# A selection moved from VectorE to ScalarE and GpSimd, and the inner dimension of an expansion turned round, in a four-layer attention kernel

## Chip, cores and metric

The kernel runs on one core of a Trainium2 chip. The metric is the device time of one execution in microseconds (us), the median of some runs. Engines: PE is TensorE, DVE VectorE, ACT ScalarE, POOL GpSimd, SP SyncE.

## What is computed

For each of 32 batches of 128 x 1024 numbers there are four layers. The first and third are chunked self-attention layers over the context (8 heads, chunks of 64) with a residual and a layer normalisation. The second is a cross attention with LoRA weights (32 heads, width 1024). The fourth builds on geometry: for each of 1024 points of the context (first three channels of 128-channel rows, used as coordinates) it finds the 30 nearest of 1024, turns their relative coordinates into spherical ones, passes them through a three-layer perceptron with batch normalisation over everything, takes a softmax over the 30, and adds the weighted sum of the neighbours' features.

```python
idx = _knn(x_loc, k)
rel = pts[bidx, idx] - pts[:, :, None, :]
...
att = jax.nn.softmax(h[..., 0], axis=-1)
xk = x.transpose(0, 2, 1)[bidx, idx]
agg = jnp.einsum('bnkc,bnk->bnc', xk, att)
return x + agg.transpose(0, 2, 1)
```

## The kernel before

The program is written per engine, each with its own queue in hand-written order; engines meet at semaphores only. It has three stages.

**Main loop, 32 batches.** Each batch runs the first three layers. Their heads are worked in three blocks of four groups, n = 0 to 11. In a group PE computes scores, DVE takes a row maximum (`front`), ACT the exponentials, PE transposes the probabilities, ACT copies them out (`ET`), PE multiplies with the values, DVE normalises (`normalise`), PE transposes again (`outputs`), ACT copies that out (`output`, line 1008). After each block PE projects (line 758 in blocks 0 and 2, line 814 in block 1) and DVE adds the residual (lines 1369, 1405).

Between these steps DVE searches the 30 nearest neighbours of the batch (`search_round`, 32 of them, three operations of 1.2 us each on 1024 distances). The coordinates of the neighbours of the batch before are fetched in the same groups: an index is split into a low part (0 to 127) and a high part (0 to 7). A DMA spreads the low parts over all partitions, DVE compares them with the partition's number (`onehot`, line 1274), and PE multiplies the one-hot matrix with a table of coordinates (`fill`, line 636, 60 matmuls). That gives for each pair 3 coordinates x 8 possible high parts in the PSUM bank `MISC`. `consume` on DVE selects: it multiplies by the mask `hm` of the high part (line 1284) and sums over the 8 (line 1289) into `crd`. DVE does `consume` of group n-1 in group n, the last one behind the last group; PE's next `fill` waits for its `nb_used`.

POOL works in its own order: `tangents`, `norm_parts` (for the next batch's distances), `turn`, the split of the new indices, the coordinate table `ptab`, `relative`, `hm`, `sides`. Apart from `norm_parts` these are steps of the spherical coordinates.

**Perceptron.** Some 430 us, not touched.

**Aggregation, 32 batches.** The weighted sum over neighbours is computed by matmuls with one-hot matrices: an index is split into h (64 values) and l (16 values). For each half batch DVE forms weighted one-hots of l in `BA` (`weights`, line 1560, 16 operations). ACT expands them into block form `BD` (`blocks`, line 1220, four operations with a scale per partition, before each pair of chunks). DVE forms one-hots of h in `A1` (`onehots`, line 1569). PE multiplies both (`chunk`, line 918, eight chunks a batch, alternating over the banks SCA and SCB). ACT evacuates each chunk into `WT` (`columns`, line 1228), and PE forms the result from `WT` and the features, once for each half (`final`, line 931), behind chunks 1 (for the batch before) and 5. DVE adds the residual (`finish`). ACT's order is: expansion of the next pair, then the evacuations of this pair's two chunks. A chunk waits for its one-hots, its expansion, and the evacuation of the chunk two before.

```python
src = BA[half].rearrange("r l (h p) -> r h p l", h=2)[:, :, 32 * w:32 * w + 32, :]
for j in range(4):
    last = A(BD[v % 2][:, :, :, :, j], src, ACT.Copy, scale=blockmask[0:GROWS, j:j + 1])
```

## Time and profile before

| | us |
|---|---|
| median of 3 runs (8473.54 to 8476.95) | 8475.44 |
| the profiled execution | 8474.7 |
| its span, first to last instruction | 8472.9 |
| PE busy | 6946.1 |
| DVE busy | 6525.4 |
| ACT busy | 4626.7 |
| POOL busy | 1642.5 |
| mean granted clock of TensorE | 0.858 of 2.4 GHz |

Busy time is a sum over stages with different limits. The main loop takes the first four fifths of the span, the aggregation the last sixth; what a change is worth must be read in the stage where it lies. Matmuls are pipelined, so a busy PE isn't one at its peak.

### The profile page before, as it was taken

Reading aid. Unit: us, or ns where it says so; the run is one execution under the profiler, and the core shown is the slowest. Engines: PE = TensorE matmul, PEld = TensorE weight load, DVE = VectorE, ACT = ScalarE, POOL = GpSimd, SP = SyncE. Lnnn points to the kernel's source line nnn. Section 1 sums busy time; section 2 is a strip of 40 time slices with the busy share of each in tenths; the row PEclk is TensorE's granted clock in tenths of the full one; section 3 lists DMA queues with packets and bytes.
Section 4 is the critical chain, followed back from the end, with each engine's and each line's share of the span. In section 5 each row is a group of like instructions: output and inputs, shape, how many; then the busy total and the mean of one; then the engine's idle time right before and its main releaser. Section 6 shows DMA issues by size and latency. Waiting matters only on the chain.

```text
span 8472.9 us, 200463 instructions
## 1 busy us (share of the span) xinstructions
PE 6946.1 (82%) x79422; PEld 4984.0 (59%) x79422; DVE 6525.4 (77%) x9276; ACT 4626.7 (55%) x9523; POOL 1642.5 (19%) x1863
## 2 busy tenths in 40 slices
PE   8888888888888888888888888888888585888888
PEld 5555555555555555555555555555555332777777
DVE  5888888888888888888888888888888557666665
ACT  2444454554444444454444444444444225999999
POOL 1222222222222222222222222222222300010010
PEclk9888888888888888888888888888888797899999
DMA  2111111111111111111111111111111302222221
GB/s 97 57 54 54 54 54 54 58 56 54 54 54 54 57 58 59 64 54 57 57 57 57 54 54 54 54 54 57 57 57 55 101 16 54 55 55 55 65 55 49
DMA packets 295401, 481.05 MB, mean 57 GB/s; under 512 B 103250, under 2 KB 216034, under 8 KB 293698
## 3 DMA queue, kind: packets, MB, share of 16 engines
q1 hardware_dynamic: 240205, 372.00, 14.7%
q10 hardware_dynamic: 54133, 94.55, 3.5%
q8 instruction: 706, 11.57, 0.6%
q14 instruction: 357, 2.92, 0.1%
HBM read 393.25 MB, written 73.25 MB: 55 GB/s over the span
## 4 chain that ended last, share of the span: by engine, by line
PE 29%; DVE 27%; ACT 22%; issue 19%; DMA 1%; ACTq 1%; DVEq 1%; POOL 0%; SPq 0%; POOLq 0%
ACT arena L1220 8%; DVE m L1318 8%; DVE pd L1324 7%; PE SCA L814 5%; ACT S L1013 4%; ACT kexp L1055 3%; PE MISC L636 3%; DVE gat L1274 2%; DVE prod L1284 2%; DVE mx L1330 1%; PE TP L716 1%; PE TP L806 1%; PE SCB L654 1%; ACT reg L1065 1%; ACT reg L1228 1%
## 5 line engine op out<-in xcount | busy, mean ns | idle before, releaser
L1318 DVE MAX8 m<-pd 128x8 f32<-128x1024 f32 x1024 | 1249.1, 1220 | 207.2 <-ACT pd L988 94.2
L1322 DVE FIND_INDEX8 idx<-m,pd 128x8 uint32<-128x1024 f32 x1024 | 1248.3, 1219 | 0.0
L1324 DVE MATCH_REPLACE8 pd<-m,pd 128x1024 f32<-128x1024 f32 x768 | 928.5, 1209 | 0.0
L1569 DVE TENSOR_TENSOR gat<-maskT,con 120x2048 f32<-120x2048 f32 x256 | 580.9, 2301 | 295.6 <-PE SCA L918 281.0
L611 PE MATMUL PD<-arena 128*128 128x512 f32 x1028 | 695.8, 766 | 133.0 <-ACT pd L988 110.7
L636 PEld LDWEIGHTS MISC<-ptab,gat 128*128 128x128 bf16 x23400 | 667.7, 99 | 81.2 <-issue 44.4
L1013 ACT ACTIVATE S<-SCA,mx 128x64 f32<-128x64 f32 (+1 forms) x2560 | 571.4, 365 | 242.7 <-DVE mx L1330 242.7
L636 PE MATMUL MISC<-ptab,gat 128*128 128x24 bf16 x23400 | 664.7, 176 | 33.1 <-DVE gat L1274 23.1
L402 POOL CAST mb<-arena 96x1024 bf16<-96x1024 f32 x33 | 34.1, 1034 | 3078.8 <-ACT arena L978 3078.8
L1013 ACT ACTIVATE S<-SCB,mx 128x64 f32<-128x64 f32 (+1 forms) x2560 | 575.4, 399 | 0.0
L1330 DVE TENSOR_REDUCE mx<-SCA 128x16 f32<-128x1024 f32 (+1 forms) x192 | 235.1, 1225 | 429.1 <-PE SCA L739 420.6
L1220 ACT ACTIVATE arena<-S,con 120x1024 f32<-120x1024 f32 x256 | 542.6, 2375 | 17.4 <-DVE S L1560 17.4
L1220 ACT ACTIVATE arena<-pd,con 120x1024 f32<-120x1024 f32 x256 | 545.4, 2396 | 0.0
L988 ACT ACTIVATE pd<-PD,xxcol 128x512 f32<-128x512 f32 x514 | 355.4, 691 | 310.9 <-PE PD L612 305.1
L918 PE MATMUL SCA<-arena,gat 120*64 120x64 f32 x8192 | 325.6, 249 | 239.3 <-ACT reg L1228 130.2
L1008 ACT ACTIVATE OT<-TP 128x256 f32<-128x256 f32 x384 | 151.6, 395 | 657.8 <-PE TP L681 657.8
L783 PE MATMUL SCA<-reg,arena 128*128 128x128 f32 x4096 | 465.9, 276 | 35.6 <-ACT reg L1112 35.6
L783 PEld LDWEIGHTS SCA<-reg,arena 128*128 128x128 f32 x4096 | 459.8, 192 | 43.2 <-ACT reg L1112 43.2
L654 PE MATMUL SCA<-con,S 128*128 128x128 f32 x1536 | 234.4, 302 | 292.2 <-ACT S L1013 292.2
L750 PE MATMUL TP<-reg,ET 128*64 128x34 f32 x8192 | 389.7, 262 | 100.1 <-DVE on L1356 100.1
L750 PEld LDWEIGHTS TP<-reg,ET 128*64 128x64 f32 x8192 | 359.4, 180 | 179.2 <-issue 177.3
L918 PEld LDWEIGHTS SCA<-arena,gat 120*64 120x64 f32 x8192 | 307.0, 162 | 263.8 <-issue 263.8
(265 smaller groups left out, 15053.1 us busy)
## 6 DMA issues: line engine op xcount, KB each, us to landing
gat<-low_scratch SPq DMA_DIRECT2D x396, 640.0 KB, 4.3
arena<-in_ctx ACTq DMA_DIRECT2D x33, 512.0 KB, 4.0
maskT<-in_mask ACTq DMA_DIRECT2D x32, 512.0 KB
arena<-in_x ACTq DMA_DIRECT2D x32, 512.0 KB, 6.1
x_scratch<-arena ACTq DMA_DIRECT2D x32, 512.0 KB, 5.0
x3T_scratch<-arena ACTq DMA_DIRECT2D x32, 512.0 KB, 3.7
arena<-x3T_scratch SPq DMA_DIRECT2D x32, 512.0 KB, 7.1
arena<-x_scratch SPq DMA_DIRECT2D x32, 512.0 KB, 9.3
```

The lines of the kernel that those rows point to most:

```text
L611: mm(PD[:, :], ctx[:, t * P:(t + 1) * P], ctx[:, h * 512:(h + 1) * 512], start=True, stop=False)
L636: last = mm(place[:, o:o + 3 * NT], oh[n % NOH][:, kk * 256 + half * P:kk * 256 + (half + 1) * P], ptab[:, part, :, :].rearrange("p c t -> ...
L750: last = mm(TP[64 * half:64 * half + 64, (4 * b + pair) * 2 * VW:(4 * b + pair + 1) * 2 * VW], ET[:, o:o + 64], V2[:, (4 * g + 2 * b + hal ...
L783: last = mm(SC[0][:, c * P:(c + 1) * P], Wq[:, kc, c * P:(c + 1) * P], hT[:, kc, :], start=(kc == 0), stop=(kc == KC - 1))
L814: last = mm(SC[0][:, h * 512:(h + 1) * 512], OT[:, c * P:(c + 1) * P], Wo[:, c, h * 512:(h + 1) * 512], start=(c == 0), stop=(c == KC - 1))
L918: last = mm(SC[c % 2][64 * h:64 * h + 64, p * 64:(p + 1) * 64], A1[c % 2][:, h, p, :], BD[v % 2][:, h, c % 2 * 16 + p, :, :].rearrange("r ...
L1013: last = A(S[g % 2][:, r * keys:(r + 1) * keys], SC[g % 2][:, r * keys:(r + 1) * keys], ACT.Exp, bias=mx[g % 2][:, r:r + 1])
L1220: last = A(BD[v % 2][:, :, :, :, j], src, ACT.Copy, scale=blockmask[0:GROWS, j:j + 1])
L1318: step(V.max(m, buf[:, :]))
L1322: last = V.max_index(idx[:, t, 8 * r:8 * r + 8], m, buf[:, :])
L1324: step(V.match_replace(buf[:, :], m, buf[:, :], -3.0e38))
L1569: V.tensor_tensor(A1[c % 2], low[:, :, 16 * part:16 * part + 16].unsqueeze(3) .broadcast_to([GROWS, 2, 16, HV]), iota64[0:GROWS, :].unsque ...
```

## The change

It has two parts that don't depend on each other.

The first is in the aggregation. `BA` is stored with l innermost instead of outermost, and `BD` with (j, l) instead of (l, j). The expansion on ACT then reads and writes runs of 16 floats. The price of it moves: DVE's `weights` write with a step of 16 floats, the chunk's columns in PSUM come in another order, and ACT's evacuation reads PSUM with a step of 16 floats and writes runs of 64.

The second is in the main loop. `consume` leaves DVE. ACT copies group n's products from `MISC` into `prod` (`pick`, in group n, behind the exponentials of the next group), and POOL multiplies by `hm` and adds the 8 up in three steps, 4, 2 and 1 wide. POOL does groups 0 to 3 before `tangents`, 4 to 10 before `norm_parts`, and 11 behind it. `pick` waits until POOL has finished the group before. The layout of `prod` and `ptab` changes so that the 3 coordinates are innermost. In the tail behind the loop DVE still does the selection, in the new layout.

```diff
-        ptab = sb("ptab", [P, 3, 3, NT], bf16)
+        ptab = sb("ptab", [P, 3, NT, 3], bf16)
-        prod = sb("prod", [P, 2 * OHROWS, 3, NT])
+        prod = sb("prod", [P, 2 * OHROWS, NT, 3])
...
-        BD = [free[0:GROWS, n * UC * 64:(n + 1) * UC * 64].rearrange("r (h p l j) -> r h p l j", h=2, p=32, l=LV)
+        BD = [free[0:GROWS, n * UC * 64:(n + 1) * UC * 64].rearrange("r (h p j l) -> r h p j l", h=2, p=32, l=LV)
...
-        BA = [w[0:GROWS, :].rearrange("r (l c) -> r l c", l=LV) for w in (S01, pd01)]
+        BA = [w[0:GROWS, :].rearrange("r (c l) -> r c l", l=LV) for w in (S01, pd01)]
...
+            def consume(i, n):
+
+                if n == 0:
+                    pool.wait_ge(hm_ready, i + 1)
+                pool.wait_ge(nb_used, i * GROUPS + n + 2)
+                settle(pool)
+                count = [0]
+
+                def done(ins):
+                    count[0] += 1
+                    ins.then_inc(pick_step, 1)
+                    pool.wait_ge(pick_step, i * 3 * GROUPS + 3 * n + count[0])
+                    settle(pool)
+
+                pairs = slice(2 * n * OHROWS, 2 * (n + 1) * OHROWS)
+                done(G_.tensor_tensor(prod[:, :, :, :], prod[:, :, :, :], hm[:, pairs, :].unsqueeze(3)
+                                      .broadcast_to([P, 2 * OHROWS, NT, 3]), ALU.mult))
+                done(G_.tensor_tensor(prod[:, :, 0:4, :], prod[:, :, 0:4, :], prod[:, :, 4:8, :], ALU.add))
+                done(G_.tensor_tensor(prod[:, :, 0:2, :], prod[:, :, 0:2, :], prod[:, :, 2:4, :], ALU.add))
+                G_.tensor_tensor(crd[:, n * OHROWS:(n + 1) * OHROWS, :, :].rearrange("p k a c -> p (k a) c"),
+                                 prod[:, :, 0, :], prod[:, :, 1, :], ALU.add).then_inc(crd_done, 1)
...
                 pool.wait_ge(split_ready, i + 1)
+                for n in range(4):
+                    consume(i, n)
                 tangents(i)
+                for n in range(4, GROUPS - 1):
+                    consume(i, n)
                 norm_parts(i + 1)
+                consume(i, GROUPS - 1)
                 turn(i)
...
+                        def pick(n):
+                            act.wait_ge(nb_ready, i * GROUPS + n + NOH + 1)
+                            act.wait_ge(crd_done, i * GROUPS + n + 1)
+                            A(prod[:, :, :, :].rearrange("p k t c -> p (k t c)"), MISC[:, 0:6 * OHROWS * NT],
+                              ACT.Copy).then_inc(nb_used, 1)
...
                             if g < 3:
                                 exponentials(g + 1)
+                            pick(n)
                             if g == 0:
                                 expand(3)
                             if g:
                                 output(n - 1)
...
-                src = BA[half].rearrange("r l (h p) -> r h p l", h=2)[:, :, 32 * w:32 * w + 32, :]
+                src = BA[half].rearrange("r (h p) l -> r h p l", h=2)[:, :, 32 * w:32 * w + 32, :]
                 for j in range(4):
-                    last = A(BD[v % 2][:, :, :, :, j], src, ACT.Copy, scale=blockmask[0:GROWS, j:j + 1])
+                    last = A(BD[v % 2][:, :, :, j, :], src, ACT.Copy, scale=blockmask[0:GROWS, j:j + 1])
...
-                A(WT[half][:, :, c % 4 * 16:c % 4 * 16 + 16, :].rearrange("p l c j -> p c l j"),
-                  SC[c % 2][:, :].rearrange("p (c l j) -> p c l j", l=LV, j=4), ACT.Copy).then_inc(wt_done, 1)
+                A(WT[half][:, :, c % 4 * 16:c % 4 * 16 + 16, :].rearrange("p l c j -> p l (c j)"),
+                  SC[c % 2][:, :].rearrange("p (n l) -> p l n", l=LV), ACT.Copy).then_inc(wt_done, 1)
...
-                        if n:
-                            consume(i, n - 1, MISC)
...
-                    if l:
-                        consume(i, GROUPS - 1, MISC)
...
-                    last = V.scalar_tensor_tensor(BA[half][:, l, :], Lf[par][:, cols], float(l), attT[par][:, cols],
+                    last = V.scalar_tensor_tensor(BA[half][:, :, l], Lf[par][:, cols], float(l), attT[par][:, cols],
                                                   ALU.is_equal, ALU.mult)
```

## Rows read from the trace of the kernel before

**Rows 1.** The page's first line.

```profile
span 8472.9 us, 200463 instructions
```

**Rows 2.** One batch of the main loop, and most of the aggregation, by stretch: columns below.

```profile
core 0: us, PE busy (x) PEld busy (x) DVE busy (x) ACT busy (x) POOL busy (x), PEclk, DMA share, GB/s
...
3787.00:3992.00 205.00, 170.94 (x1793) 119.79 (x1792) 167.52 (x234) 99.86 (x268) 46.04 (x53) 0.85 0.17 56
...
7280.00:8440.00 1160.00, 956.26 (x18672) 880.95 (x18666) 756.96 (x1248) 1159.87 (x698) 103.84 (x140) 0.92 0.25 58
```

**Rows 3.** The chain that ended last, two batches: start, us, what.

```profile
3704.92 14.11 PE SCA L814 x32
3909.74 14.10 PE SCA L814 x32
```

**Rows 4.** Single lines: duration in ns, least, median, most; first and last start.

```profile
L1560 DVE SCALAR_TENSOR_TENSOR S<-maskT,TP x512: 272/279/289, 7174.4 to 8404.6; 120x128 f32<-120x128 f32 x171
...
L485 POOL TENSOR_TENSOR sph<-sph,arena x34: 1196/1199/1207, 288.2 to 6821.7; 128x480 f32<-128x480 f32 x34
...
L474 POOL TENSOR_TENSOR sph<-sph,arena x34: 1194/1712/1722, 165.0 to 6768.9; 128x480 f32<-128x480 f32 x34
...
L450 POOL TENSOR_TENSOR arena<-arena x34: 690/692/694, 107.5 to 6762.6; 128x240 f32<-128x240 f32 x34
```

**Rows 5.** The timeline of a quarter batch of the aggregation: start, us, engine, [idle before].

```profile
7803.00 1.14 ACT L1228 ACTIVATE arena<-SCA 128x1024 f32<-128x1024 f32 x1
7803.86 3.25 DVE L1560 SCALAR_TENSOR_TENSOR S<-maskT,TP 120x128 f32<-120x128 f32 x16
7804.29 3.16 PE L918 MATMUL SCA<-arena,gat 120*64 120x64 f32 x64 [3.13 <-ACT arena L1228]
7804.84 8.40 ACT L1220 ACTIVATE arena<-pd,con 120x1024 f32<-120x1024 f32 x4
...
7809.72 0.48 PE L931 MATMUL PD<-arena,kexp 64*128 64x256 f32 x1
...
7813.00 1.09 ACT L1228 ACTIVATE reg<-SCA 128x1024 f32<-128x1024 f32 x1
...
7816.82 2.08 PE L918 MATMUL SCA<-arena,gat 120*64 120x64 f32 x64
7818.74 2.04 PE L918 MATMUL SCB<-arena,gat 120*64 120x64 f32 x64
```

**Rows 6.** Groups of the main loop, ACT, from 96 to 6650 us.

```profile
L1055 ACT ACTIVATE kexp<-reg,con 128x256 f32<-128x256 f32 x1024 | 447.5, 581 | 0.0
...
L978 ACT ACTIVATE arena<-PD 96x512 f32<-96x512 f32 x64 | 37.7, 588 | 8.8 <-PE PD L597 8.8
```

**Rows 7.** Groups of the aggregation: busy us, mean ns, idle before.

```profile
L1569 DVE TENSOR_TENSOR gat<-maskT,con 120x2048 f32<-120x2048 f32 x242 | 548.7, 2300 | 272.4 <-PE SCA L918 258.6 <-PE SCB L918 13.4
```

**Rows 8.** The timeline of DVE and PE in group 6 of the main loop.

```profile
3889.41 0.65 DVE L1284 TENSOR_TENSOR prod<-MISC,hm 128x480 f32<-128x480 f32 x1
3890.09 0.65 DVE L1289 TENSOR_REDUCE crd<-prod 128x60 f32<-128x480 f32 x1
3890.66 1.22 DVE L1318 MAX8 m<-pd 128x8 f32<-128x1024 f32 x1
...
3895.36 2.38 PE L806 MATMUL TP<-reg,ET 128*128 128x33 f32 x16 [2.33 <-DVE on L1356]
```

**Rows 9.** The timeline of POOL, the last of the norm parts.

```profile
3761.11 1.03 POOL L406 CAST mb<-arena 32x1024 bf16<-32x1024 f32 x1 [0.17 <-POOL arena L405]
```

**Rows 10.** The timeline of ACT and PE in group 3.

```profile
3834.11 0.52 ACT L1008 ACTIVATE OT<-TP 128x256 f32<-128x256 f32 x1
...
3839.97 1.98 PE L758 MATMUL SCA<-OT,WL 128*128 128x512 f32 x4 [0.47 <-ACT OT L1008]
```

**Rows 11.** The timeline of ACT and PE in groups 9 to 11.

```profile
3744.52 1.29 ACT L1024 ACTIVATE arena<-arena 128x1024 f32<-128x1024 f32 x1
...
3756.70 1.92 PE L750 MATMUL TP<-reg,ET 128*64 128x34 f32 x32 [2.03 <-DVE on L1356]
...
3768.08 3.78 PE L758 MATMUL SCA<-OT,WL 128*128 128x512 f32 x4 [0.47 <-ACT OT L1008]
```

17 lines of the change are left out of this document (9 added, 8 removed).

## The prediction

> **What bounds the kernel now.** I read the page first: the execution spans 8472.9 us [rows 1], and its slices change their look once, late. The views by stretch split it into two stages that matter. In one batch of the main loop PE is busy 171 of 205 us, DVE 168, ACT 100, POOL 46. In the aggregation at the end ACT is busy 1159.9 of 1160 us and PE 956 [rows 2]. The chain of waits then gives the pace of the main loop: the 14 us projection of line 814 starts 204.82 us after that of the batch before [rows 3]. Its chain passes from DVE to PE to ACT and back several times in a batch, so a microsecond taken from one engine counts only where that engine is the late one. The aggregation (from 7174 us [rows 4] to the end, 1298 us) is simpler: the timeline of ACT repeats the same thing every 10.0 us, four expansions (line 1220) and two evacuations (line 1228), without a gap, while PE stands idle 3.1 us before each second pair of chunks, waiting for ACT [rows 5]. There ACT alone sets the time, 40.0 us for a batch.
>
> **Part 1, runs of 16 in the expansions.** Four expansions of 120x1024 take 8.16 us from their start to the evacuation behind them, 2.04 us each or 2.0 ns an element [rows 5]. What sets line 1220 apart is its pattern: it reads single floats 1 KB apart and writes them 16 bytes apart. The same operation with both sides contiguous (a copy from SBUF to SBUF with a scale per partition, line 1055) does 256 elements in 447.5/1024 = 0.437 us [rows 6], so four of them 1.75 us with the fixed part counted four times. The other ACT operation of 1024 elements in this stage, the evacuation, takes 0.92 us (1.84 for two [rows 5]). After the change both sides of the expansion are runs of 16 floats. I take 1.05 us, nearer to the row of the same size. Below 1.5 us nothing hangs on it, as the walk below shows. The bounds are 0.92 and 2.04 (the pattern wasn't the cause).
>
> The Trainium skill's page "SBUF — State Buffer", section Specifications (TRN2), says that a 16-byte line needs at least two accesses in a row for full bandwidth and that every step to a new line costs. The trace agrees: one access per line goes with 2.0 ns an element. By that rule the new expansions run at full rate, which gives the same sum.
>
> The evacuation now reads PSUM in single floats 64 bytes apart and writes runs of 64. No row shows such a read on ACT. Bounds: 0.92 as now, and twice that, 1.84, which is the penalty that line 1220 shows. ACT then needs 16 x 1.05 + 8 x 0.92 = 24.2 us a batch, or 31.5 with the upper one; with 1.5 us for an expansion it would be 31.4. The same page gives PSUM lines of only 8 bytes, which speaks against this edit; by it the evacuations would take the upper value, and the batch about 32.5 us in place of 31.6.
>
> The weights of DVE (line 1560) now write single floats 64 bytes apart. A group of 16 takes 3.25 us [rows 5]; if the write costs double, about 5.4 us.
>
> So what is late next? I walk one batch from the start of chunk 0, with PE at its higher clock. A chunk takes 1.92 us, the final products with the transposes 7.1 us [rows 5], a one-hot of DVE 2.27 us [rows 7], and up to 0.15 us for each handover (evacuation over at 7804.14, chunk at 7804.29 [rows 5]). A one-hot may start only when the chunk two before is done, and chunk c needs one-hot c. Chunk 1 starts at 2.25, final and transposes run 4.2 to 11.4, chunk 2 starts at 11.45, chunk 3 at 13.4. One-hot 4 runs 13.55 to 15.85, chunk 4 starts at 15.95, chunk 5 (one-hot 5 ends at 18.1) at 18.2, the other final runs 20.2 to 27.05, chunk 6 starts at 27.1, chunk 7 at 29.05; the next one-hot 0 runs 29.2 to 31.5, and the next chunk 0 starts at 31.6. PE is busy 8 x 1.92 + 2 x 7.1 = 29.6 of the 31.6 us, DVE 8 x 2.27 + 6.5 = 24.7 and some small ones, ACT 24.2. The weights fall into both finals (2.2 to 7.6, 18.1 to 23.5 even at the double cost), where DVE has over 3 us spare, so they cost nothing; without that cover they would cost 2 us each. The longest gap of PE is 0.6 us. Now it idles 3.1 us and the chunk behind takes 3.16 us instead of 2.08 [rows 5]; the granted clock of the stage is 0.92 [rows 2], so such chunks run in part at the lower of its two levels (1.2 in place of 2.4 GHz). This goes too, and my walk counts on it. Gain 40.0 - 31.6 = 8.4 us a batch, times 32: 269 us. Bounds: 31.0 us (all handovers free) and 34 us (clock still falls once a batch): 288 and 192 us.
>
> **Part 2, the selection.** Removed from DVE: 12 pairs of multiply and reduce in a batch, 0.65 us each, 1.25 us from the start of the first to the next operation [rows 8], 15 us a batch. Added on ACT: 12 copies of 480 floats out of PSUM. The nearest row is the 512 wide copy of line 978, 0.59 us [rows 6]; I take 0.55 us, 0.5 in a stream. Added on POOL: a multiply of 480, then adds of 240, 120 and 60, each waiting for the one before (0.17 us from one to the next [rows 9]). POOL multiplies 480 in 1.20 us and 240 in 0.69 [rows 4], so 2.1 ns an element beside 0.18 us: 1.2 + 0.69 + 0.44 + 0.31 and three handovers of 0.17, 3.2 us. Upper bound 4.2: the 480 multiply of line 474 takes 1.71, and the broadcasts could add as much again. That is 38 us a batch on a POOL that is busy 46 of 205: it fits.
>
> A new wait comes with it: ACT may fill prod for group n only when POOL is done with n-1. Behind that wait in ACT's queue stands the evacuation of the last head output, and behind it PE's output projection. The groups of the three attention blocks:
>
> Block 0 (groups 0 to 3). PE sets the pace; DVE gains little. The copy of group 2 can start at 3834.1, where line 1008 stands now [rows 10]; it and the handovers last to 3834.9, POOL's 3.2 us end at 3838.1, and the copy of group 3, whose matmuls are done by then, ends at 3838.9. Outputs 2 and 3 then follow one another on ACT and PE, and the projection of line 758, now at 3839.97 [rows 10], starts 0.3 us later. Bounds: 0.2 gained, 1.3 lost (4.2 us on POOL). I take 0.3 lost.
>
> Block 1 (groups 4 to 7). Here DVE is late: PE waits 2.33 us for its normalisation [rows 8]. Two selections lie on that path, 2.5 us. PE's own work behind (values, transposes, line 636) lets through about 2.3. A one-hot of DVE can meet POOL's multiply here. I take 2.0, bounds 1.0 and 2.5. What follows is PE's 14 us projection, so this carries on.
>
> Block 2 (groups 8 to 11). The copy of group 8 lies on ACT's path, in front of the expansion and the square of line 1024 [rows 11], and costs 0.5 us. PE waits 2.03 us for DVE at 3756.70; that wait shrinks by 1.25 - 0.5 = 0.75, and then PE's own chain up to the output projection limits, with about 0.3 more from the last normalisation. The selection in front of line 1369 goes as well, and the projection becomes the late one. I take 1.3. Bounds 0.5 and 3.5: the projection takes 3.78 us here and 1.98 in block 0 [rows 10, 11], after a wait of PE that the change shortens.
>
> POOL's moved steps: the norm parts (8 us, now over at 3762.1 [rows 9]) have to wait for selection 10, to about 3762. They are then done at 3770, and PE asks for them behind the projection of line 758, at 3771; selection 11 and the last turn end at 3776, and POOL is next needed by the last search at 3778. Cover of 1 to 2 us, so nothing; at 4.2 us a selection this cover is gone and it costs up to 0.5 us. The tangents wait for DVE's reciprocal between selections 3 and 4, 10 us before group 4 has data: nothing. The tables written in another order cost the same. The tail's 12 selections stay on DVE.
>
> Sum: 2.0 + 1.3 - 0.3 = 3.0 us a batch, 96 us over 32.
>
> **The total.** 8472.9 - 269 - 96 = 8107.9 us of span; the profiled execution had 1.8 us beside its span, 8109.7, and the median of the runs stands 0.7 above that execution: 8110 us.
>
> **The rivals.** (a) POOL and DVE get in each other's way. Line 474 on POOL takes 1.19 us at best and 1.71 usually [rows 4], so something holds it. With 38 us more of POOL's work among the groups, a one-hot of DVE in block 1 could start 1 us late and ACT's copies later: the lower bounds of the three blocks, 1.0 + 0.5 - 1.3 = 0.2 us a batch, 6 us in place of 96, 8200 us. Against it: only 2 or 3 of the 12 selections meet a one-hot where DVE is late. Chance 0.16. The Trainium skill, same page, section "SBUF: two separate sides", makes this an exclusive lock for the whole instruction, against DVE's operations with two SBUF inputs or in a fast mode; by it the time would go towards the 8200 of this rival.
> (b) The clock stays up in blocks 1 and 2, because PE's waits of 2 us shrink: the upper bounds, 2.5 + 3.5 + 0.2 = 6.2 us a batch, 8474.7 - 269 - 198 = 8008. Against: PE's other waits in the loop stay. Chance 0.12.
> (c) The aggregation takes 34 us a batch, by slower evacuations and a falling clock together: 8110 + 77 = 8187. Against: PE's longest gap in the walk is 0.6 us. Chance 0.10.
> (d) The expansions don't get faster, since something else holds them: 8474.7 - 96 = 8379. Against it stand the contiguous copies [rows 6]. Chance 0.04.
> (e) Slower than before: POOL's selection lasts so long that ACT waits for it in every block. Two copies follow one another by 3 us in block 0, and by my placing of them by about 6 in the others. To eat 269 + 96 us, 11.4 us a batch and 3.8 a block, a selection must last some 5 + 3.8 = 8.8 us against my 3.2; from there it decides. At 10 us the time would be 8474.7 + 3 x 1.2 x 32 = 8590. Chance 0.03.
> My forecast (8110, own range 8050 to 8170) has 0.55.
>
> **How the numbers follow.** The range 7990 to 8220 takes in the forecast, (a), (b) and (c), and leaves out (d) and (e). 0.2% is 17 us, about what a measurement of this kernel can tell. Only (e) is slower; faster 0.96, same 0.01, slower 0.03.
>
> **What the profile after would show.** Line 1220 near 1.0 us each and ACT with gaps in the aggregation; PE near 9 tenths there, granted clock near 1, batch 31.6 us. In the loop, the projection of line 814 every 201.8 us, copies of 0.55 us on ACT, four POOL operations summing to 3.2 us. I would be wrong if line 1220 stays near 2 us, if one-hots start behind POOL's operations, or if ACT's copies wait for POOL in block 1 or 2.

## The result, and the profile after

The changed kernel takes 8265.39 us (median of 4 runs, 8259.28 to 8271.05) beside 8476.19 for the one before: ratio 0.9751, interval 0.9734 to 0.9768, 211 us less. I had forecast 8110 with a range of 7990 to 8220, so the direction was right and the size was not: 155 us of the forecast gain are missing. The profiled execution took 8271.05 us.

First the page: the span, the busy times and the granted clock over 40 slices.

```profile
span 8269.3 us, 204463 instructions
...
PE 6884.4 (83%) x79422; PEld 4925.1 (60%) x79422; DVE 6179.9 (75%) x8508; ACT 4307.4 (52%) x9907; POOL 2685.8 (32%) x3399
...
PEclk9888888888888888888888888888888779899999
```

DVE lost 346 us of work and ACT 319, POOL took on 1043. Where the time stands is read from two rows: the weights of the aggregation (their first start divides the stages) and the projection of line 842 (814 before), each with durations in ns and its first and last start.

```profile
L1591 DVE SCALAR_TENSOR_TENSOR S<-maskT,TP x512: 359/388/416, 7113.1 to 8214.0; 120x128 f32<-120x128 f32 x171
...
L842 PE MATMUL SCA<-arena,OT x1024: 590/592/1061, 217.7 to 6529.7; 128*128 128x512 f32 x171
```

The aggregation begins at 7113.1 instead of 7174.4 [rows 4], so all that lies ahead of it gained 61 us, where 96 were forecast. From there to the end it takes 8269.3 - 7113.1 = 1156.2 instead of 1298.5, 142 us less, where 269 were forecast. So 127 us are missing in the aggregation and 35 in the main loop (together 162 of span against the forecast 8107.9; 155 by the medians).

The windows over most of the aggregation, which answer to [rows 2]:

```profile
core 0: us, PE busy (x) PEld busy (x) DVE busy (x) ACT busy (x) POOL busy (x), PEclk, DMA share, GB/s
7260.00:8200.00 940.00, 834.51 (x16712) 760.87 (x16710) 707.83 (x1120) 639.41 (x626) 144.04 (x130) 0.95 0.27 64
```

ACT fell from all of the stage to 68%, PE rose from 82% to 89%: as forecast, PE is the late engine now. The groups of ACT and DVE there (busy us, mean ns, idle before):

```profile
L1255 ACT ACTIVATE arena<-pd,con 120x1024 f32<-120x1024 f32 x210 | 223.8, 1139 | 0.0
...
L1263 ACT ACTIVATE arena<-SCB 128x1024 f32<-128x1024 f32 x52 | 53.1, 1021 | 45.0 <-PE SCB L946 45.0
...
L1600 DVE TENSOR_TENSOR gat<-maskT,con 120x2048 f32<-120x2048 f32 x210 | 486.1, 2353 | 146.7 <-PE SCA L946 138.2 <-PE SCB L946 8.6
L1591 DVE SCALAR_TENSOR_TENSOR S<-maskT,TP 120x128 f32<-120x128 f32 x416 | 97.0, 387 | 0.0
```

The time from one batch's transposes to the next alternates: 33.10 us, then 36.7 to 41.1 (from 7265.50 on: 40.79, 33.10, 39.11, 33.10, 38.63, and so on to the end), 35.9 in the mean. The walk gave 31.6 for all. The timeline of a quick batch shows the first part of the difference (start, us, engine, idle before):

```profile
7743.29 4.49 DVE L1600 TENSOR_TENSOR gat<-maskT,con 120x2048 f32<-120x2048 f32 x2 [0.97 <-PE SCA L946]
7743.78 1.21 PE L946 MATMUL SCB<-arena,gat 120*64 120x64 f32 x35
7745.92 2.08 PE L946 MATMUL SCA<-arena,gat 120*64 120x64 f32 x64 [0.92 <-DVE gat L1600]
...
7745.97 4.26 ACT L1255 ACTIVATE arena<-pd,con 120x1024 f32<-120x1024 f32 x4
7748.02 2.08 PE L946 MATMUL SCB<-arena,gat 120*64 120x64 f32 x64
```

Ahead of chunks 0 and 4, so once in four chunks, PE idles 0.92 us for a one-hot. The first of the two one-hots takes 2.29 us by itself and ends at 7745.58, and the chunk starts 0.34 us later, not 0.10 as in the walk. The same wait stood in the trace of the kernel before, at one chunk 4:

```profile
7722.22 2.29 DVE L1569 TENSOR_TENSOR gat<-maskT,con 120x2048 f32<-120x2048 f32 x1 [0.96 <-PE SCA L918]
...
7724.84 2.08 PE L918 MATMUL SCA<-arena,gat 120*64 120x64 f32 x64 [0.92 <-DVE gat L1569]
```

At chunk 1 of the quick batch PE waits once more, for another reason. One-hot 0 holds up an operation of POOL that took 0.74 us in the median before, and this one then holds up one-hot 1, which ends after 2.82 us instead of 2.29:

```profile
7759.40 5.03 DVE L1600 TENSOR_TENSOR gat<-maskT,con 120x2048 f32<-120x2048 f32 x2 [3.28 <-PE SCA L946]
7759.87 2.40 POOL L592 TENSOR_TENSOR maskT<-ctxT 120x256 f32<-120x256 f32 x1 [0.18 <-POOL ctxT L591]
...
7764.66 2.09 PE L946 MATMUL SCB<-arena,gat 120*64 120x64 f32 x64 [0.55 <-DVE gat L1600]
```

The start of a slow batch, 20 us before the first of these timelines, shows the second part:

```profile
7721.06 5.03 DVE L1600 TENSOR_TENSOR gat<-maskT,con 120x2048 f32<-120x2048 f32 x2 [3.51 <-PE SCA L946]
7721.22 2.71 POOL L592 TENSOR_TENSOR maskT<-ctxT 120x256 f32<-120x256 f32 x1 [0.18 <-POOL ctxT L591]
...
7726.17 2.19 PE L946 MATMUL SCA<-arena,gat 120*64 120x64 f32 x36 [3.41 <-DVE gat L1600]
7728.98 1.76 PE L946 MATMUL SCA<-arena,gat 120*64 120x64 f32 x28 [0.62 <-issue]
7730.52 3.12 PE L946 MATMUL SCB<-arena,gat 120*64 120x64 f32 x64
```

PE idles 3.41 us where it idled 0.92, breaks off in the middle of the chunk without a wait ("issue"), and the next chunk takes 3.12 us instead of 2.08, at the lower clock. The timeline names DVE's one-hot as what ended the 3.41 us, but that one-hot had ended at 7723.35, 2.8 us before the chunk starts. This is where TensorE's loop of two batches jumps back. All 14 jumps look like this: PE idles 3.2 to 4.8 us (3.9 in the mean), breaks off after 36 of 64 matmuls (0.8 in the mean), and these batches take 39.0 us in the mean.

In the main loop, the groups of POOL's selection (lines 509 to 513), ACT's copy and DVE's one-hots, over the stretch 2400 to 6500 us:

```profile
L509 POOL TENSOR_TENSOR prod<-prod,hm 128x480 f32<-128x480 f32 x242 | 256.1, 1058 | 1845.8 <-ACT prod L1041 1738.7 <-issue 107.2
L511 POOL TENSOR_TENSOR prod<-prod 128x240 f32<-128x240 f32 x242 | 182.4, 754 | 43.2 <-POOL prod L509 43.2
L512 POOL TENSOR_TENSOR prod<-prod 128x120 f32<-128x120 f32 x242 | 111.3, 460 | 43.2 <-POOL prod L511 43.2
L513 POOL TENSOR_TENSOR crd<-prod 128x60 f32<-128x60 f32 x242 | 87.5, 362 | 43.2 <-POOL prod L512 43.2
...
L1041 ACT ACTIVATE prod<-MISC 128x480 f32<-128x480 f32 x242 | 154.6, 639 | 60.5 <-POOL crd L513 32.4 <-PE MISC L664 28.0
...
L1309 DVE TENSOR_SCALAR gat<-gat,con 128x2560 bf16<-128x2560 bf16 x243 | 243.9, 1004 | 0.0
```

The selection on POOL takes 1.06 + 0.75 + 0.46 + 0.36 and three handovers of 0.18, 3.17 us: the forecast 3.2. The copy takes 0.64 us, not 0.55. But a one-hot takes 1004 ns in the mean, and ACT waits for POOL. The one-hots of the kernel before, same stretch:

```profile
L1274 DVE TENSOR_SCALAR gat<-gat,con 128x2560 bf16<-128x2560 bf16 x240 | 210.8, 878 | 0.0
```

Single one-hots show how. The timeline in block 2 (groups 8 to 11) of one batch:

```profile
2902.26 1.04 POOL L509 TENSOR_TENSOR prod<-prod,hm 128x480 f32<-128x480 f32 x1 [5.72 <-ACT prod L1041]
2902.28 1.70 DVE L1309 TENSOR_SCALAR gat<-gat,con 128x2560 bf16<-128x2560 bf16 x1
...
2903.48 1.06 POOL L511 TENSOR_TENSOR prod<-prod 128x240 f32<-128x240 f32 x1 [0.18 <-POOL prod L509]
2904.07 1.66 PE L664 MATMUL MISC<-ptab,gat 128*128 128x24 bf16 x60
```

POOL starts 0.02 us ahead, and DVE's 0.88 us one-hot takes 1.70; then POOL's add of 0.69 takes 1.06, since the one-hot is running. Over all 396 one-hots the median is 878 ns and the longest 1742, and the 174 that have no POOL operation beside them take at most 0.89 us; of the 12 in this batch ten took 0.88 and two 1.70 and 1.73, and PE stands behind them. The Trainium skill's page "SBUF — State Buffer", section "SBUF: two separate sides", calls the port pair of the two engines an exclusive lock, held for the whole instruction by whichever starts first; the trace agrees, with 0.88 against 1.70 us here.

The same happens at a place that the forecast didn't look at, the last step of the first layer norm. The changed kernel's timeline:

```profile
2994.58 1.83 DVE L1414 TENSOR_SCALAR X<-X,mv,rstd 128x1024 f32<-128x1024 f32 x1
...
2994.66 1.20 POOL L475 TENSOR_TENSOR sph<-sph,arena 128x480 f32<-128x480 f32 x1 [0.18 <-POOL arena L472]
```

and that of the kernel before:

```profile
2826.57 0.81 DVE L1383 TENSOR_SCALAR X<-X,mv,rstd 128x1024 f32<-128x1024 f32 x1
...
2826.74 1.72 POOL L474 TENSOR_TENSOR sph<-sph,arena 128x480 f32<-128x480 f32 x1 [0.18 <-POOL arena L471]
```

There POOL's product began 0.17 us behind DVE's step and waited (1.72); now it begins 0.08 us behind DVE's recorded start and DVE waits (1.83). It does so in every batch: 1826 to 1840 ns in all 32, against 811 to 814 before. This is the 1.71 against 1.19 us of line 474 in [rows 4], seen from the other side.

How a batch of the main loop divides, in means over 29 or 30 batches from the timelines of PE (a stretch in us, and the granted clock in it; of the last two columns more below):

| stretch | before | after | `ln_first` | `copy_only` |
|---|---|---|---|---|
| line 842 to block 2 | 32.3 | 32.6 | 32.7 | 33.4 |
| block 2, to its output projection | 31.1 (0.87) | 32.9 (0.73) | 32.3 (0.75) | 29.8 (0.76) |
| to block 0 | 41.2 | 41.0 | 41.0 | 40.9 |
| block 0, to its output projection | 30.7 (0.69) | 28.0 (0.82) | 28.7 (0.79) | 28.2 (0.78) |
| that projection and the first layer norm, to line 811 | 13.6 | 14.9 | 13.9 | 14.7 |
| line 811 to block 1 | 21.1 | 22.0 | 21.5 | 22.1 |
| block 1, to line 842 | 34.8 (0.76) | 31.6 (0.81) | 32.0 (0.80) | 29.3 (0.91) |
| sum | 204.8 | 203.0 | 202.1 | 198.4 |

Block 0 gained 2.7 us and block 1 gained 3.2, but block 2 lost 1.8 and the stretches around line 811 lost 2.2. In the kernel before, every step from the fourth on was 204.7 to 204.9 us; now they run from 197.6 to 207.7. The loop has also become uneven from one trace to the next. Seven kernels here (the changed one, `p2_only`, `agg_pe3`, `agg_dve3`, `agg_flat`, `onehot_12`, `three_buf`) have this same main loop, and their aggregations begin at 7096 to 7129 us. So a difference of less than some 30 us in the main loop can't be read from one trace, while a stretch of the table can: the projection with the layer norm has 14.9 to 15.0 us in all seven.

### The profile page after: what moved, and what is told of

It is laid out like the page before. It is cut to its first block, busy times and chain, and to the rows that moved or that the text cites. A ratio compares the mean times of both kernels' runs of the same rounds, so it can differ in the third digit from the quotient of the medians.

```text
span 8269.3 us, 204463 instructions
## 1 busy us (share of the span) xinstructions
PE 6884.4 (83%) x79422; PEld 4925.1 (60%) x79422; DVE 6179.9 (75%) x8508; ACT 4307.4 (52%) x9907; POOL 2685.8 (32%) x3399
## 4 chain that ended last, share of the span: by engine, by line
PE 54%; DVE 16%; ACT 15%; issue 10%; POOL 2%; DMA 1%; ACTq 1%; DVEq 0%; SPq 0%; POOLq 0%
ACT S L1047 6%; PE SCA L842 6%; PE PD L959 5%; PE SCA L811 4%; PE MISC L664 4%; PE SCA L946 3%; DVE m L1353 3%; ACT kexp L1090 3%; PE TP L834 3%; DVE pd L1359 3%; PE SCB L946 2%; PE PD L639 2%; PE SCA L682 2%; PE SCA L786 2%; PE TP L778 2%
## 5 line engine op out<-in xcount | busy, mean ns | idle before, releaser
L1353 DVE MAX8 m<-pd 128x8 f32<-128x1024 f32 x1024 | 1249.3, 1220 | 210.8 <-ACT pd L1016 99.0
L509 POOL TENSOR_TENSOR prod<-prod,hm 128x480 f32<-128x480 f32 x384 | 406.1, 1057 | 2928.8 <-ACT prod L1041 2762.2
L639 PE MATMUL PD<-arena 128*128 128x512 f32 x1028 | 660.8, 730 | 149.7 <-ACT pd L1016 127.5
L811 PE MATMUL SCA<-reg,arena 128*128 128x128 f32 x4096 | 500.7, 288 | 35.6 <-ACT reg L1147 35.6
L682 PE MATMUL SCA<-con,S 128*128 128x128 f32 x1536 | 276.4, 340 | 281.4 <-ACT S L1047 281.4
L842 PE MATMUL SCA<-arena,OT 128*128 128x512 f32 x1024 | 471.7, 621 | 0.0
L682 PEld LDWEIGHTS SCA<-con,S 128*128 128x128 f32 x1536 | 232.6, 177 | 372.7 <-ACT S L1047 341.7
L1365 DVE TENSOR_REDUCE mx<-SCB 128x16 f32<-128x1024 f32 (+1 forms) x192 | 234.6, 1222 | 286.5 <-PE SCB L767 252.4
L1090 ACT ACTIVATE kexp<-reg,con 128x256 f32<-128x256 f32 x1024 | 445.4, 572 | 0.0
L1309 DVE TENSOR_SCALAR gat<-gat,con 128x2560 bf16<-128x2560 bf16 x396 | 397.4, 1003 | 60.3 <-DMA gat<-low_scratch 60.3
L561 POOL TENSOR_SCALAR hm<-hif 128x240 bf16<-128x240 f32 x256 | 398.6, 1709 | 8.0
```

Of the source, the lines that this page charges most:

```text
L639: mm(PD[:, :], ctx[:, t * P:(t + 1) * P], ctx[:, h * 512:(h + 1) * 512], start=True, stop=False)
L682: last = nc.tensor.transpose(SC[g % 2][:, b * 512 + j * P:b * 512 + (j + 1) * P], S[g % 2][:, b * 512 + j * P:b * 512 + (j + 1) * P], ident)
L811: last = mm(SC[0][:, c * P:(c + 1) * P], Wq[:, kc, c * P:(c + 1) * P], hT[:, kc, :], start=(kc == 0), stop=(kc == KC - 1))
L842: last = mm(SC[0][:, h * 512:(h + 1) * 512], OT[:, c * P:(c + 1) * P], Wo[:, c, h * 512:(h + 1) * 512], start=(c == 0), stop=(c == KC - 1))
L1090: last = A(kexp[:, o:o + 256], kT[:, g * 256:(g + 1) * 256], ACT.Copy, scale=headmask[:, h:h + 1])
L1353: step(V.max(m, buf[:, :]))
```

## The experiments

The ratios stand against the kernel before. Medians are of 4 runs (5 for `ln_first`, 6 for `best_ln`).

**1. Each part alone.** `p1_only` is the kernel before with the layouts of `BA`, `BD` and the two ACT views; `p2_only` is the changed kernel with these undone.

> The kernel before with the expansion part alone. If the two parts simply add, the aggregation keeps its 142 us gain and the main loop its old pace of 204.8 us: 8476 - 142 = 8334 us. If the moved selection also disturbs the tail or the start of the aggregation, this kernel gains more than 142 us, towards 8320.

> The kernel before with the selection part alone. If the parts add: 8476 - 61 = 8415 us, the projection of line 842 every 203.1 us on the mean with unequal steps (197.7 to 207.7), and 40.0 us a batch in the aggregation. If the uneven steps came from the other part of the change, which has no work in the loop, they are gone here.

Measured: 8329.53 us (0.9826, 0.9810 to 0.9843) and 8421.05 (0.9937, 0.9920 to 0.9953). The parts are worth 147 and 55 us, and 147 + 55 = 202 of 211: they add, to within the spread of `p2_only` (8413 to 8439). The miss has a part in each stage, then.

**2. Whose jump makes the slow batch?** `agg_pe3` gives TensorE a loop over six batches in the aggregation, `agg_dve3` gives it to DVE.

```diff
-            with pe.Fori(0, NB // 2 - 1) as pair:
-                for odd in (1, 0):
-                    aggregate(pair * 2 + (2 - odd), odd, pair + (1 - odd))
+            with pe.Fori(0, (NB // 2 - 1) // 3) as three:
+                for m in range(3):
+                    for odd in (1, 0):
+                        aggregate(three * 6 + (2 * m + 2 - odd), odd, three * 3 + (m + 1 - odd))
```

> The changed kernel, with six batches instead of two in the body of PE's aggregation loop, so 5 jumps instead of 15, and DVE's loop as it was. Theory J (PE's own jump is what costs 3.4 us of gap, a break of 0.6 us and chunks at the lower clock, some 5.4 us each): 10 jumps less, 8265 - 54 = 8211 us, and the slow chunk 0 appears only once in six batches. Theory D (DVE's jump costs it: PE waits for one-hots that come late): 8265 us, no change. Theory C (the clock alone falls once a pair whatever the loop is): 8265 us.

> The same with DVE's loop unrolled threefold and PE's as it was. Theory J: 8265 us, no change. Theory D: 8211 us. Theory C: 8265 us.

Measured: 8271.62 (0.9761, 0.9740 to 0.9782) and 8270.96 (0.9767, 0.9739 to 0.9795). Neither gained. With DVE's loop unrolled every second batch was still slow, so it isn't DVE's jump. With TensorE's, the slow batch moved to the new jump, but three batches of six were slow: the spacing of the transposes was 33.10, 33.15, 33.10, 33.64, 36.84, 44.73 us. Together that is 16 us over 6 x 33.1, against 3 x 5.6 = 17 in the pair loop. (Over all 30 steps it is 67 us against 84, so the aggregation of this trace is 14 us shorter; its main loop is 13 us longer, within the unevenness above.) The new slow batches hold breaks in the middle of a chunk, ahead of the jump, as this timeline of `agg_pe3` shows:

```profile
7561.54 1.85 PE L946 MATMUL SCB<-arena,gat 120*64 120x64 f32 x56
7568.15 0.45 PE L946 MATMUL SCB<-arena,gat 120*64 120x64 f32 x8 [4.76 <-issue]
```

56 of 64 matmuls are done and nothing holds the last 8, yet PE stops for 4.76 us. A chunk needs no further operand, so I read this as TensorE lacking instructions, which left two theories for the next run. The DMA records of the traces support the reading. They have a queue (q8) that brings instructions in packets of 16 KB. In the changed kernel, from 7722.8 to 7726.2, between PE's stop and its next chunk, it shows (packets, MB, share of 16 engines)

```profile
q8 instruction: 1, 0.02, 2.0%
```

and this one packet, the only one of any queue, starts at 7723.16, 0.4 us after the stop and 3.0 us before PE resumes. At all 14 jumps a packet starts 0.3 to 1.0 us after the stop, and PE resumes 2.8 to 4.4 us behind its start. At each of the 14 breaks in chunk 0 PE resumes 2.2 to 2.9 us behind the start of one. In the 4.76 us of `agg_pe3` none had started since 7553.51; one starts at 7565.60, and PE resumes at 7568.15. The records don't name the engine that a packet is for, so it is the timing that ties them to PE.

**3. No jump.** `agg_flat` writes TensorE's 30 middle batches out.

```diff
-            with pe.Fori(0, NB // 2 - 1) as pair:
-                for odd in (1, 0):
-                    aggregate(pair * 2 + (2 - odd), odd, pair + (1 - odd))
+            for i in range(1, NB - 1):
+                aggregate(i, i % 2, i // 2)
```

> The changed kernel with TensorE's 30 middle batches of the aggregation written out without any loop (the loop of 15 pairs had a jump ahead of every second batch). Theory J (the slow batch of every pair, 38.6 to 41 us beside 33.1, is the jump, with the low clock behind it): all batches at 33.1, so 8265 - 15 x 5.6 = about 8180. Theory F (TensorE runs out of instructions in a stretch this dense, jump or no jump, as with the loop of six batches that had breaks in the middle of chunks): breaks stay or grow, batch mean 35 to 36, 8250 to 8275. I hold F likelier after the loop of six.

Measured: 8192.98 us (0.9679, 0.9656 to 0.9702), 72 us less, and J's 8180 nearly reached. 22 batches have 32.9 to 33.1 us; two episodes of four and three batches (33.6, 33.7, 38.6, 36.0 and 33.4, 36.7, 35.6) remain. The windows, 7300 to 8000 us, columns as above:

```profile
7300.00:8000.00 700.00, 644.19 (x13276) 583.87 (x13278) 560.26 (x901) 508.42 (x501) 97.67 (x100) 0.99 0.29 69
```

The clock came up to 0.99 with the pauses gone. The Trainium skill, "Runtime: NRT & Kernel Launch", section "Instruction fetch mechanics", says that a taken branch breaks the prefetch of instructions and that its target may have to be fetched before execution goes on. These runs agree that the jump is what costs, 72 of the 5.6 x 15 = 84 us counted in the slow batches (in the traces the aggregation fell from 1156.1 to 1085.4 us, 71). The six breaks in the two episodes, 0.6 to 3.3 us long, end like those at the jumps, 2.7 to 3.0 us behind the start of an instruction packet. Why these packets start late no run here shows.

**4. The quick batch.** `onehot_12` leaves out a quarter of the columns of each one-hot of the aggregation from batch 1 on.

```diff
-                V.tensor_tensor(A1[c % 2], low[:, :, 16 * part:16 * part + 16].unsqueeze(3)
+                m = 16 if isinstance(i, int) else 12
+                V.tensor_tensor(A1[c % 2][:, :, 0:m, :], low[:, :, 16 * part:16 * part + m].unsqueeze(3)
```

> The changed kernel, whose one-hots in the aggregation (batches 1 on) leave out a quarter of their columns, so that each takes VectorE some 1.7 us instead of 2.2 to 2.3; TensorE's work is as before (it reads what the first batch left in the columns left out). Theory H (the undisturbed batch is 33.1 and not the 31.6 that I walked because one-hot and handover, 2.2 + 0.3, are longer than a chunk, and TensorE waits 0.9 us ahead of c0 and c4 and 0.5 ahead of c1): the batch comes to 31.2 to 32, 31 x 1.5 = 45 us less, about 8220, or more if the clock stays higher. Rival: the 33.1 is set by ScalarE's expansions or TensorE's own pace: no change, 8260 to 8270.

Measured: 8236.04 us (0.9710, 0.9694 to 0.9726). The quick batches went from 33.10 to 31.0 to 31.4 us, as H has it, while the slow ones (37.3 to 40.0, 38.5 in the mean) gained 0.5. In the trace the aggregation is 37 us shorter and the uneven main loop 7 longer, which fits the 29 us of the medians. So one-hot and handover set the quick batch, the jump the slow one.

**5. A third one-hot buffer.** `three_buf` is `agg_flat` with a third place for a one-hot (in two free pieces, so two operations), `a_done` as before, DVE waiting one chunk less, its loop over six batches.

```diff
+        A1.append([w.rearrange("r (p c) -> r p c", p=16) for w in (free[0:GROWS, 14336:15360], reg[0:GROWS, 4096:5120])])
...
-                dve.wait_ge(chunk_ready, i * 8 + c + 3)
+                dve.wait_ge(chunk_ready, i * 8 + c + 2)
```

> The changed kernel with TensorE's part of the aggregation written out without a loop (8193 us) and a third buffer for VectorE's one-hots (every third one in two operations on two free places), so that one-hot c may be made while TensorE is still at chunk c-2; VectorE's loop over six batches instead of two. Theory H (33.1 us a batch is the handover between one-hots and chunks, as the one-hots cut to three quarters showed with 31.3): batches of 31.2 to 31.8, 31 x 1.5 = 45 us less, 8140 to 8155. Rival: the chain through ScalarE's expansions or the weights holds it then: 8175 to 8195.

Measured: 8099.1 us (0.9561, 0.9545 to 0.9577), 94 us less than `agg_flat`, twice what I expected. Its windows:

```profile
7300.00:8000.00 700.00, 694.98 (x14833) 638.72 (x14831) 619.22 (x1059) 562.34 (x555) 160.50 (x115) 1.00 0.32 77
```

PE is busy for 99% of the stage at the full clock, and the twelve batches from 7324 to 7688 us take 30.0 to 31.2 us. With the handovers gone there is little left but PE's own work, 29.6 us in the walk. Two of the twelve batches (31.2 and 31.0) have a break in a chunk, of 0.99 and 0.86 us; the long ones of `agg_flat`, up to 3.3 us, are absent.

**6. What does the selection still cost?** `no_select` leaves out the selection of the main loop, `copy_only` keeps only ACT's copy, `last_add` the copy and POOL's fourth operation. The cut of `last_add`, and then what stands for the whole of `consume` in the other two:

```diff
-                done(G_.tensor_tensor(prod[:, :, :, :], prod[:, :, :, :], hm[:, pairs, :].unsqueeze(3)
-                                      .broadcast_to([P, 2 * OHROWS, NT, 3]), ALU.mult))
-                done(G_.tensor_tensor(prod[:, :, 0:4, :], prod[:, :, 0:4, :], prod[:, :, 4:8, :], ALU.add))
-                done(G_.tensor_tensor(prod[:, :, 0:2, :], prod[:, :, 0:2, :], prod[:, :, 2:4, :], ALU.add))
```

```diff
             def consume(i, n):
                 pool.wait_ge(nb_used, i * GROUPS + n + 2)
+                pool.sem_inc(crd_done, 1)
```

In `no_select` ACT's copy is a mere count of `nb_used` as well.

> The changed kernel with the coordinate selection left out in the main loop (no copy on ScalarE, no products and sums on GpSimd; only their semaphores are counted), so the limit of what taking it off VectorE can give. Theory L (VectorE's relief is worth the 3.0 us a batch that I forecast and more, but GpSimd's operations beside VectorE's, with one-hots of 1003 ns instead of 879, and ScalarE's waits eat half of it): at least 1.3 us a batch comes back, 8265 - 32 x 1.3 = 8223 or lower, one-hots at 880 ns. Theory P (TensorE's own work and clock are the bound by now, VectorE's relief is worth 1.7 us a batch whoever does the selection): 8250 to 8265.

> The changed kernel with GpSimd doing only the last of the four operations of each group's selection (the product and the first two adds left out, 2.2 of 2.4 us of GpSimd's time), ScalarE's copy kept. Theory L with the collisions on GpSimd's side: most of what leaving all out gives, 8235 or lower, one-hots near 880 ns. Theory L with ScalarE's copy as the costly part: near 8265. Theory P: 8250 to 8265, no difference from leaving all out.

> The changed kernel with ScalarE's copy of each group kept and all four of GpSimd's selection operations left out. Without any selection 8117, with the copy and GpSimd's last add 8167. Theory C (ScalarE's copies of 0.64 us x 12 lie before work that TensorE waits for): 8150 to 8170. Theory G (the last add on GpSimd, held up by and holding up VectorE, makes the difference): 8115 to 8130.

Measured: 8117.45 us (0.9572, 0.9557 to 0.9588), 8167.35 (0.9630, 0.9614 to 0.9646) and 8126.97 (0.9584, 0.9569 to 0.9600). So 148 us still hang on the selection: 40 on POOL's last and shortest add, 98 on its other three operations, and 10 on ACT's copies, which is too little to tell from nothing (8114.67 to 8136.00 beside 8110.23 to 8124.29). Theory P, that PE is the bound whoever selects, has fallen. One-hots of `last_add` and `copy_only`:

```profile
L1296 DVE TENSOR_SCALAR gat<-gat,con 128x2560 bf16<-128x2560 bf16 x245 | 222.5, 908 | 0.0
```
```profile
L1291 DVE TENSOR_SCALAR gat<-gat,con 128x2560 bf16<-128x2560 bf16 x249 | 220.3, 885 | 37.6 <-DMA gat<-low_scratch 37.6
```

**7. Waiting for POOL, or working beside it?** `early_free` lets POOL's first add write to the unused tail of the one-hot tile, so that ACT may refill `prod` after two operations. `free_first` does the last add first and then the other three on data of their own.

```diff
-                done(G_.tensor_tensor(prod[:, :, 0:4, :], prod[:, :, 0:4, :], prod[:, :, 4:8, :], ALU.add))
+                done(G_.tensor_tensor(part[:, :, :, :], prod[:, :, 0:4, :], prod[:, :, 4:8, :], ALU.add))
...
-                            act.wait_ge(crd_done, i * GROUPS + n + 1)
+                            act.wait_ge(pick_step, i * 3 * GROUPS + 3 * n + 1)
```

and in `free_first`:

```diff
-                done(G_.tensor_tensor(prod[:, :, :, :], prod[:, :, :, :], hm[:, pairs, :].unsqueeze(3)
-                                      .broadcast_to([P, 2 * OHROWS, NT, 3]), ALU.mult))
-                done(G_.tensor_tensor(prod[:, :, 0:4, :], prod[:, :, 0:4, :], prod[:, :, 4:8, :], ALU.add))
-                done(G_.tensor_tensor(prod[:, :, 0:2, :], prod[:, :, 0:2, :], prod[:, :, 2:4, :], ALU.add))
                 G_.tensor_tensor(crd[:, n * OHROWS:(n + 1) * OHROWS, :, :].rearrange("p k a c -> p (k a) c"),
                                  prod[:, :, 0, :], prod[:, :, 1, :], ALU.add).then_inc(crd_done, 1)
+                twice = con[:, 0:60].rearrange("p (k c) -> p k c", c=3).unsqueeze(2).broadcast_to([P, 2 * OHROWS, NT, 3])
+                done(G_.tensor_tensor(part[:, :, :, :], twice, hm[:, pairs, :].unsqueeze(3)
+                                      .broadcast_to([P, 2 * OHROWS, NT, 3]), ALU.mult))
...
```

> The changed kernel in which GpSimd's first add of each group of the selection writes to a buffer of its own (the tail of the one-hot tile), so that ScalarE's next copy may start after two of GpSimd's four operations instead of after all four, 1.2 us earlier; GpSimd's work is the same. Without three of the four operations the kernel gained 98 us, without the whole selection 148. Theory W (of those, the 57 us of ScalarE's waits for the product's buffer are the cause): these waits fall below 15 us and the time by 30 to 60, about 8220. Theory K (GpSimd's operations beside VectorE's lengthen one-hots, 1004 ns beside 908 and 881, whoever waits): waits of ScalarE fall, the time stays within 15 us of 8265.

> The changed kernel in which GpSimd does the last add of each group first, straight from ScalarE's copy, and frees the buffer, and then does the product and the two other adds on data of their own (output 480, 240 and 120 elements of bf16 in the tail of the one-hot tile; their result is not used): GpSimd as busy as in the changed kernel, ScalarE never waiting for it. Theory W: nearly all of the 98 us that leaving the three operations out gave, 8165 to 8190. Theory K: little of it, 8235 to 8265, with one-hots still near 1000 ns. I give W and K even chances, and a part from each is possible: then the split is what the run measures.

Measured: 8261.7 us (0.9741, 0.9725 to 0.9758) and 8249.4 (0.9735, 0.9718 to 0.9751). The row of ACT's copy in `early_free`:

```profile
L1043 ACT ACTIVATE prod<-MISC 128x480 f32<-128x480 f32 x244 | 158.9, 651 | 29.3 <-PE MISC L666 29.3
```

ACT no longer waits for POOL at all, and the time fell by 4 us, in `free_first` by 16, both within the unevenness of the main loop. Theory W has fallen: what costs is that POOL works, not the wait for `prod` that the prediction walked through block by block. Theory K is right in the time, but not in what was to go with it, one-hots near 1000 ns. In `free_first` POOL is nearly as busy as before (its operations of a group take 2.5 instead of 2.6 us), yet its operations meet fewer one-hots:

```profile
L1311 DVE TENSOR_SCALAR gat<-gat,con 128x2560 bf16<-128x2560 bf16 x244 | 226.6, 929 | 0.0
```

929 ns instead of 1004, with 878 undisturbed, and next to no time came back. Twelve one-hots of 1004 instead of 885 ns (`copy_only`) make 1.4 us a batch, where the two kernels lie 4.3 apart, and DVE's other operations in the loop add 0.1 us to that. So the lengthened operations of DVE are some third of it by their own time.

The windows over 29 batches of the changed kernel and then of `copy_only` show where the difference lies (columns as above); the matmuls are the same 51970:

```profile
624.50:6515.00 5890.50, 4940.32 (x51970) 3464.54 (x51969) 4504.42 (x6061) 3054.92 (x8120) 2231.36 (x2871) 0.84 0.17 56
```
```profile
615.10:6369.90 5754.80, 4879.48 (x51970) 3403.75 (x51969) 4458.60 (x6062) 3051.87 (x8120) 1313.23 (x1479) 0.86 0.18 57
```

Of the 135.7 us between them, PE's idle time is 74.9 (2.6 us a batch) and its busy time 60.8 (2.1 a batch), the same matmuls at a mean granted clock of 0.84 instead of 0.86.

**8. The layer norm.** `ln_first` holds POOL's product in the tangents until DVE's first layer norm is done.

```diff
+                if not isinstance(i, int):
+                    pool.wait_ge(xl_done, i * 3 + 1)
+                settle(pool)
                 done(G_.tensor_tensor(sph[:, 1:3, :], sph[:, 1:3, :], rel_zy, ALU.mult))
```

> The changed kernel in which GpSimd's product of 480 elements in the tangents waits until VectorE's first layer norm of the batch is done. In the kernel before, the layer norm's last step took 0.81 us and the product 1.72; in the changed one the product starts first, takes 1.20, and the step 1.83. Theory N (whichever starts first holds the other up, and the step is on the way from the first chunk attention to TensorE's transposes): the step goes back to 0.81, the stretch from the second output projection to the next queries from 14.9 to about 13.8, and the time by about 1.0 us x 32 = 32 us, 8225 to 8245. Rival (TensorE's clock or another wait takes it back): 8255 to 8270.

Measured: 8238.75 us (0.9713, 0.9696 to 0.9730), 27 us less, inside theory N's 8225 to 8245. In its trace the aggregation begins at 7091.1 us, 22 us earlier and just below the 7096 to 7129 of the seven kernels above. The step in `ln_first`:

```profile
L1417 DVE TENSOR_SCALAR X<-X,mv,rstd 128x1024 f32<-128x1024 f32 x20 | 16.2, 812 | 0.7
```

It is back at 812 ns, and the stretch from the output projection to line 811 at 13.9 us, 1.0 below all seven. A wait that was added made this stretch faster, and the kernel by about as much.

**9. The parts together.** `best` is `three_buf` with the early release; `best_ln` adds the wait of `ln_first`.

> Both at once: TensorE's aggregation without a loop, three one-hot buffers, and GpSimd's first add to a buffer of its own. If the parts add: the time of the three buffers less what the early release gives, 8100 to 8150 (theory W), or within 10 us of that with three buffers alone (theory K).

> The fastest so far (8066: TensorE's aggregation without a loop, three one-hot buffers, GpSimd's first add to its own buffer) with the wait for the first layer norm ahead of GpSimd's product. Theory N: 30 us less, 8030 to 8045. Rival: 8055 to 8070.

Measured: 8066.15 us (0.9537, 0.9504 to 0.9570) and 7994.4 (0.9433, 0.9418 to 0.9448; its runs spread from 7919.56 to 8060.49, wider than those of any other kernel here). Both are faster than the changed kernel and the one before. `best` is 33 us below `three_buf`, where theory K allowed 10 and theory W nothing below 8100; in the traces the aggregation is the same (988.5 and 989.7 us) and the main loop 33 us shorter, which is about its unevenness. That `best_ln` gained 72 us, where its edit was worth 27 alone, stays unexplained. The execution whose trace was kept is its slowest (8060.49 us at a mean granted clock of 0.865; the others had 0.878 to 0.893), and that one is 7 us behind the traced one of `best`.

## Why the prediction was wrong

**Right.** The first part of the argument held as written: the pattern of line 1220 was its cost (8.16 us down to 4.26 for four, where 4.2 was forecast), ACT left the path, and PE became the late engine. The weights (387 ns instead of 279, 3.7 us for 16) stayed under cover. The evacuation reads PSUM in single floats 64 bytes apart in 1.02 us for 1024 elements, no slower than the 1.09 to 1.14 of [rows 5], so the price that the prediction worked out from the 8-byte PSUM lines of the Trainium skill's page "SBUF — State Buffer", section Specifications (TRN2), did not come up: for ACT's read the measurement decides. POOL's 3.2 us were right, ACT's 0.55 were 0.64.

**Wrong, the aggregation: "up to 0.15 us for each handover" and "the longest gap of PE is 0.6 us", so 31.6 us a batch.** The quick batch is 33.1, and (33.1 - 31.6) x 31 = 46 us. The walk had PE wait for a one-hot at the same chunks, but mis-sized the waits. Ahead of chunks 0 and 4 the step is 0.4 us longer each: the handover from a one-hot to a chunk is 0.34 us, where the walk has 0.10 and my bound of 0.15 came from ACT's evacuation, although the trace before shows this very wait (0.92 us at 7724.84), and a chunk ends 0.13 us later than I had it. Ahead of chunk 1 it is 0.4 longer because one-hot 1, held up by POOL's line 592, takes 2.82 us. The two finals make another 0.4 (7.11 us, and 7.47 with the transposes, between the chunks before and behind them, where the walk has 6.9 and 7.25), and ahead of chunk 5 0.15 come off. The cut one-hots (31.0 to 31.4) and the third buffer (30.0) confirm that it is the one-hots that PE waits for.

**Wrong, the same walk: it has no jump in it.** Every second batch has 36.7 to 41 us, 5.6 more on average and 84 us in 15 pairs. At a jump PE idles 3.9 us in the mean where it otherwise idles 0.9, so 3.0 are the pause itself, and the break in chunk 0 adds 0.8. Both had been there in the kernel before. The pause was hidden behind PE's waits for ACT: PE idled 4.4 us ahead of chunk 0 with a jump and 4.3 without one. The break shows in 6 of its 14 jumps, as here:

```profile
7707.15 1.76 PE L918 MATMUL SCA<-arena,gat 120*64 120x64 f32 x28 [1.49 <-issue]
```

The remaining 2 us are the clock, granted at 0.54 from 7726.0 to 7733.4, behind the pause; with PE's idle times of 0.92 us in the quick batches it stayed at 1.00. `agg_flat` took 72 us of it back. 46 + 84 = 130, against 127 missing. The clock, on whose rise "my walk counts", did rise, from 0.92 to 0.95, and to 0.99 and 1.00 when the pauses went. Rival (c), 34 us a batch by a falling clock, named 77 of these 127 us; at 35.9 the batch was beyond even that. No rival alone reaches the measured 8265 (closest is (a) with 8200). (a) and (c) at once, which the prediction did not add up, would have been 8110 + 90 + 77 = 8277.

**Wrong, the main loop: 3.0 us a batch, measured 61/32 = 1.9.** The step that failed is that of the blocks, each of which I walked by the one wait that I could see. Block 0 gained 2.7 instead of losing 0.3, block 1 gained 3.2 instead of 2.0, and block 2 lost 1.8 instead of gaining 1.3. Outside of the blocks 1.3 were lost in the first layer norm and 0.9 behind line 811, where the prediction had nothing. Rival (a), POOL and DVE in each other's way, was the right mechanism, and I gave it 0.16 with the reason that only 2 or 3 of the 12 selections meet a one-hot where DVE is late. So it is, two of 12 in the batch shown, but I priced the rival by the lower bounds of the blocks, mostly delays of ACT's copies, and the time that ACT waits for POOL is worth 4 us by `early_free`, no more than the unevenness. Without POOL's four operations the loop would have gained 4.3 us a batch more (`copy_only`), mostly in block 2 (32.9 to 29.8) and block 1 (31.6 to 29.3).

**Open.** The one-hots that POOL holds up, 1.4 us a batch, don't make these 4.3 us by themselves, and `free_first`, with less than half of it, gained only 16 us. PE's busy time, so the clock, carries 2.1 of it. The blocks show the same against the kernel before: in block 2 the clock was granted at 0.87 before and 0.73 after, and PE's busy time there rose from 25.4 to 28.6 us, while block 0 went from 0.69 to 0.82 and from 28.6 to 24.9. So what block 0 gained beyond the forecast, and what block 2 lost, are in the main busy time at another clock, for which the walk has no term. But `copy_only` has 0.76 in block 2 and is quick there. How delays of under 1 us on POOL and DVE turn into waits and a lower clock was not separated.

## What to carry to other kernels

When a fix takes the late engine off a stage, walk the next engine with its own handovers and its own loop jump, not with those of the engine that is leaving; a jump that was free behind another engine's wait may be the largest term afterwards. Before moving work to GpSimd, list VectorE's operations on the critical path of the kinds that were held up here (next section), everywhere in the loop, and see which GpSimd operation will be running when each starts: one that starts a tenth of a microsecond sooner can double an instruction, and a wait on GpSimd can be the cure. The most that taking work off an engine can give is what an experiment that leaves it out altogether says; run that first.
